# Weights loaded in 128-byte runs and turned by VectorE in a two-layer recurrent and attention kernel

## The reference

```python
xn = layernorm(x)
# layer 0: a recurrent mixer whose states start at zero
xi = xn @ W_in.T                                   # 512 x 256
y  = sum(C_real * B_real * xi - C_imag * B_imag * xi, axis=-1)
s  = xn + rmsnorm(y @ W_out.T) * norm_w
# layer 1: causal attention, qkv 256 x 768, o_proj 256 x 256
s  = softmax(mask(q @ k.T / 16)) @ v @ o_proj + xn # on layernorm(xn) * gamma + beta
# both layers: the gate, with H = 1024
g  = silu( fwht( silu(xn @ W1.T) * (xn @ W3.T) ) @ W2.T )
x  = x + s * g
```

## Time and profile before

| | |
|---|---|
| median of 3 runs | 363.39 us (362.97 to 363.65) |
| the profiled execution's own time | 363.3 us |
| its span | 361.5 us |
| what lies around the span | 1.8 us |
| TensorE busy | 355.8 us, 98% of the span |
| VectorE busy | 250.6 us, 69% |
| ScalarE busy | 169.2 us, 47% |
| GpSimd busy | 100.8 us, 28% |
| granted clock of TensorE | 0.999 of full speed |

### The profile page before, as it was taken

One profiled execution on the slowest core, in us unless ns is written; L12 is line 12 of the kernel. 1 busy time (PEld: TensorE's weight loads), 2 busy tenths in 40 slices (PEclk: granted clock), 3 DMA queues, 4 the chain that ended last, 5 costly groups with the idle time before them and its releaser, 6 DMA issues.

```text
span 361.5 us, 5052 instructions
## 1 busy us (share of the span) xinstructions
PE 355.8 (98%) x1821; PEld 301.5 (83%) x1821; DVE 250.6 (69%) x481; ACT 169.2 (47%) x335; POOL 100.8 (28%) x126
## 2 busy tenths in 40 slices
PE   7999999999999999999999999999999999999996
PEld 4878888888888888888988878888888888888896
DVE  5669965886489647868568894788646887356645
ACT  2865371355135623554275544644446354454510
POOL 2154410246014723467506030060300603004000
PEclk9999999999999999999999999999999999999999
DMA  7995110525145623440242401424204332054001
GB/s 239 287 320 198 60 59 0 176 58 170 35 133 159 190 74 117 120 145 0 72 134 67 141 0 60 151 54 126 81 30 160 74 117 88 0 190 111 20 3 58
DMA packets 42336, 38.63 MB, mean 107 GB/s; under 512 B 5700, under 2 KB 41800, under 8 KB 42312
## 3 DMA queue, kind: packets, MB, share of 16 engines
q1 hardware_dynamic: 42168, 38.25, 34.8%
q10 hardware_dynamic: 144, 0.07, 0.1%
HBM read 24.09 MB, written 14.22 MB: 106 GB/s over the span
## 4 chain that ended last, share of the span: by engine, by line
PE 94%; DMA 3%; DVE 1%; SPq 1%; issue 0%; ACT 0%
PE GU L362 19%; PE GU L363 19%; PE GU L364 19%; PE O L362 8%; PE O L363 8%; PE O L364 8%; DMA stage<-in_L_ffn_W 3%; PE O L369 1%; PE T L369 1%; PE O L433 1%; PE T L362 1%; PE T L364 1%; PE T L363 1%; PE O L519 1%; PE O L518 1%; PE O L517 1%
## 5 line engine op out<-in xcount | busy, mean ns | idle before, releaser
L730 ACT ACTIVATE hf<-GU 128x512 f32<-128x512 f32 x64 | 38.2, 599 | 80.3 <-DVE hid L854 55.8
L1001 DVE TENSOR_TENSOR hf<-hf,GU 128x512 f32<-128x512 f32 x64 | 43.6, 681 | 32.5 <-PE GU L364 27.1
L362 PE MATMUL GU<-XT,W1T 128*128 128x512 f32 x128 | 50.8, 397 | 0.0
L364 PE MATMUL GU<-XT,W1T 128*128 128x512 f32 x128 | 49.9, 390 | 0.0
L363 PE MATMUL GU<-XT,W1T 128*128 128x512 f32 x128 | 49.9, 390 | 0.0
L362 PE MATMUL GU<-XT,W3T 128*128 128x512 f32 x128 | 49.9, 390 | 0.0
L364 PE MATMUL GU<-XT,W3T 128*128 128x512 f32 x128 | 49.8, 389 | 0.0
L363 PE MATMUL GU<-XT,W3T 128*128 128x512 f32 x128 | 49.8, 389 | 0.0
L854 DVE TENSOR_TENSOR hid<-hf,hid 128x512 fp32r<-128x512 f32 x64 | 48.2, 754 | 1.2 <-ACT hid L661 0.8
L362 PE MATMUL O<-hid,W2hi 128*128 128x512 f32 x112 | 44.0, 393 | 0.0
L363 PE MATMUL O<-hid,W2hi 128*128 128x512 f32 x112 | 43.7, 390 | 0.0
(11 more groups left out here) (204 smaller groups left out, 741.2 us busy)
## 6 DMA issues: line engine op xcount, KB each, us to landing
stage<-in_L_ffn_W SPq DMA_DIRECT2D x24, 256.0 KB, 5.6
swap_rows<-GX SPq DMA_DIRECT2D x7, 512.0 KB, 3.6
sT<-swap_rows SPq DMA_DIRECT2D x28, 128.0 KB, 2.7
swap_gate<-GX SPq DMA_DIRECT2D x7, 512.0 KB, 2.9
sT<-swap_gate SPq DMA_DIRECT2D x28, 128.0 KB, 2.7
swap_p<-PX SPq DMA_DIRECT2D x4, 640.0 KB, 3.2
PL<-swap_p SPq DMA_DIRECT2D x16, 160.0 KB, 3.2
swap_w<-GX SPq DMA_DIRECT2D x4, 512.0 KB, 2.9
```

The lines of the kernel that those rows point to most:

```text
L362: pe.matmul(o, lhs(0), rhs(0), start=start, stop=False)
L364: return pe.matmul(o, lhs(1), rhs(0), start=False, stop=stop)
L730: act.activation(hf[:, c % 2, :], GU[:, c % 2, 0, :], ACT.Silu).then_inc(silu_done, 1)
L1001: dve.tensor_tensor(hf[:, c % 2, :], hf[:, c % 2, :], GU[:, c % 2, 1, :], ALU.mult).then_inc(mul_done, 1)
```

## The change

- W1 and W3 of pairs 1 to 7, W2 of layer 1, W_out and qkv are loaded by `load_blocks`: four DMAs for each, every one to 32 partitions, in runs of 32 numbers (128 bytes), so that the 32x32 blocks land where the transposed matrix has them. A W1 or W3 half of a pair is 4 DMAs of 512 runs, W_out 4 of 1024, qkv 4 of 1536 and W2 of layer 1 4 of 2048.
- VectorE then turns each block in place (`turn`, `turn_w2`, `turn_wout`, `turn_wqkv`; all of them instructions of L827). The transposes by TensorE of pairs 1 to 3 (W1, W3), of W_out and qkv and of layer 1's W2 are gone, and so are `w_turn`, `move_w` and `swap_w`. Pair 0 and the W2 of layer 0 stay as they were.
- GpSimd makes the lo parts of W1 and W3 from the stage (`pair_lo`, L1220) and those of layer 1's W2 (`nat_lo`, L1231); ScalarE makes the hi parts from SBUF.
- Nine small loads (five ssm arrays, W_in, norm_w, gamma, beta) are issued by ScalarE instead of SyncE. W_in is scaled by ScalarE.
- `small_m` comes after up chunk 7 in place of before it, `w2_hi` before the hi part of MR, layer 1's Hadamard matmuls stand after chunk 6 of groups 1 and 2 and after chunk 1 of groups 2 and 3, the butterflies of layer 1 in groups 2 and 3.
- SyncE loads the rest of X, pairs 4 and 5 and layer 1's W2 before the row exchange of group 1.

```diff
+            def load_blocks(to, src, done):
+                blocks = src.rearrange("(d b) (c q a) -> q b c d a", b=Q, q=QUADS, a=Q)
+                for q in range(QUADS):
+                    sp.dma_start(to[q * Q:(q + 1) * Q].rearrange("b (c d a) -> b c d a", d=D // Q, a=Q), blocks[q]).then_inc(done, 16)
...
+            def reload_w(i):
+                for w in (0, 1):
+                    sp.wait_ge(wx_lo, 2 * (i - 3) + w + 1)
+                    load_w(i, w)
...
+            reload_w(PAIRS)
+            reload_w(PAIRS + 1)
+            load_blocks(U2[1][:, :, :].rearrange("p c d -> p (c d)"), W2[1], w2_loaded)
             move_rows(1)
```

TensorE, the head and the groups of layer 0:

```diff
                 up_chunk(0, 0, 1, True)
-                head_hadamard(1)
-                head_pair(2)
-                head_pair_w2(2)
                 up_chunk(0, 0, 2, True)
+                hadamard(1)
+                pair_w2(2)
                 up_chunk(0, 0, 3, True)
-                head_hadamard(2)
-                head_pair(3)
-                head_pair_w2(3)
                 up_chunk(0, 0, 4, True)
+                hadamard(2)
+                pair_w2(3)
                 up_chunk(0, 0, 5, True)
-                head_hadamard(3)
-                small_natural()
+                hadamard(3)
+                small_gb()
                 up_chunk(0, 0, 6, True)
+                up_chunk(0, 0, 7, True)
                 small_m()
-                up_chunk(0, 0, 7, True)
                 small_av()
...
-                    if c == 2:
+                    if c == 1 and n > 1:
                         pe.wait_ge(gateT_ready, 2 * n)
-                        next_pair_w2(PAIRS + (0, 2, 3)[n - 1])
-                    if c == 4:
-                        next_hadamard(PAIRS + (0, 2, 3)[n - 1])
...
+                        hadamard(PAIRS + 2 * n - 3)
+                    if c == 6 and n < 3:
+                        pe.wait_ge(gateT_ready, 2 * n)
+                        hadamard(PAIRS + 2 * n - 2)
```

VectorE and ScalarE:

```diff
+            def in_place(part):
+                blocks = part.rearrange("p (f a) -> p f a", a=Q)
+                return dve.transpose(blocks, blocks)
+
+            def turn(i, w):
+                dve.wait_ge(stage_loaded[i % 2][w], landed(i))
+                in_place(stage[:, i % 2, w, :]).then_inc(w_turned, 1)
...
-                    last = dve.tensor_scalar(rows2[n % 2][:, t, :], X[:, bass.ds(x_at + t, 1), :].rearrange("p a d -> p (a d)"),
-                                             mv[:, t, 0:1], rstd[:, t:t + 1], ALU.subtract, ALU.mult)
+                    last = dve.scalar_tensor_tensor(rows2[n % 2][:, t, :], X[:, bass.ds(x_at + t, 1), :].rearrange("p a d -> p (a d)"),
+                                                    mv[:, t, 0:1], rstd[:, t:t + 1].broadcast_to([P, D]), ALU.subtract, ALU.mult)
...
+            def pair_hi(i):
...
+                    hi(WT[:, 0, :, cols], stage[:, i % 2, w, :].rearrange("p (k h) -> p k h", k=KC), w_turned, 2 * (i - 1) + w + 1, w_hi)
```

More of the change, by code:

```diff
@@ L164, in two_block_kernel, with landed @@
         xT = [[XT[:, a, k, :] for k in range(KC)] for a in (0, 1)]
[L165 to L177, removed]
+        def landed(i):
+            return 16 + 64 * (i // 2) if i % 2 == 0 else 64 * (i // 2 + 1)
         def blocks_of(a, c0, c1):
@@ L306, in _ @@
-            load_pair(0, 2, stage[:, 0, :, :], stage_loaded[0])
-            for i, m in enumerate((A_theta, B_real, B_imag, C_real, C_imag)):
-                sp.dma_start(ssm[:, i, :, :], m.rearrange("c (a p) s -> p (c a) s", p=P)).then_inc(small_loaded, 16)
-            sp.dma_start(win[:, :, :], W_in.rearrange("(a p) k -> p a k", p=P)).then_inc(small_loaded, 16)
-            sp.dma_start(wout[:, :, :], W_out.rearrange("(a p) n -> p a n", p=P)).then_inc(small_loaded, 16)
-            sp.wait_ge(w2_tr, 2)
@@ L397, in head_pair_w2, with pair_w2 @@
-            def head_pair_w2(i):
+                    pe.wait_ge(stage_loaded[0][w], 16)
+                    src = stage[:, 0, w, :].rearrange("p (a k) -> p a k", a=2)
+                    transposes(GU[:, 0, w, :], [src[:, a, k * P:(k + 1) * P] for k in range(KC) for a in (0, 1)]).then_inc(w_tr, 1)
+            def pair_w2(i):
                 if i:
                     pe.wait_ge(w2nat_ready, i)
-                pair_w2_transposes(i, stage[:, i % 2, :, :], stage_loaded[i % 2], 16 * (i // 2 + 1))
@@ L402, in next_pair_w2 @@
-            def next_pair_w2(i):
-                pe.wait_ge(w2nat_ready, i)
-                pair_w2_transposes(i, stage[:, i % 2, :, :], stage_loaded[i % 2], 16 * (i // 2 + 1))
-            def next_hadamard(i):
-                pe.wait_ge(u_ready, i)
-                pair_hadamard(i, w2nat)
-            def head_hadamard(i):
+                pe.wait_ge(stage_loaded[i % 2][2], 16 * (i // 2 + 1))
+                src = stage[:, i % 2, 2, :].rearrange("p (a h) -> p a h", a=2)
+                transposes(O[:, 0, :], [src[:, a, c * P:(c + 1) * P] for c in (0, 1) for a in range(KC)]).then_inc(w2_tr, 1)
@@ L420, in small_natural, with small_gb @@
+            def small_gb():
                 pe.wait_ge(small_loaded, 16 * N_SMALL)
[L421 to L423 removed]
                 pe.wait_ge(w2nat_ready, PAIRS)
@@ L679, in pair_u, with nat_hi @@
                 act.activation(U[l][:, 2 * j:2 * j + 2, :].rearrange("p a d -> p (a d)"), O[:, 1, :], ACT.Copy, scale=float(H) ** -0.5).then_inc(u_ready, 1)
-            def nat_hi(i, nat):
-                if not (isinstance(i, int) and i == 0):
+            def nat_hi(i):
+                if i:
                     act.wait_ge(h_done, i)
-                hi(nat[:, 0, :, :].rearrange("p a d -> p (a d)"), O[:, 0, :], w2_tr, i + 1, w2nat_hi)
-            def small_hi(first, n, wait, value, done):
-                for q in range(n):
-                    dst, src = first[q]
-                    hi(dst, src, wait, value + q, done)
+                hi(w2nat[:, 0, :, :].rearrange("p a d -> p (a d)"), O[:, 0, :], w2_tr, i + 1, w2nat_hi)
             def w2_hi(l):
```

328 lines of the change are left out of this document (156 added, 172 removed).

## The result

The changed kernel took 381.37 us (median of six runs, 380.0 to 384.65) against 363.33: 1.052 times as long (95% interval 1.046 to 1.057). Its profiled execution took 384.6 us by its own time, 21.3 more than that of before; it was one of the two longest of the six, so what is read from it lies some 3 us above the median.

A forecast was written before the change was run, and what follows sets the result against it. The prediction took TensorE, busy 98% of the span, as the bound. Waits of 9.6 us against a gain of 6.45 made +3.15, so 363.4 + 3.1 = 366.5 us, range 361.8 to 376.5.

The forecast's parts named there:

- lost in full: On TensorE: work removed from its program is won in full, each wait put into it lost in full.
- at about 52: SyncE's queue ahead of group 1's row exchange: through at about 52 us, at 0.84 ns a run, so in time.
- chain c: End of the head: small_av waits for VectorE's turns of qkv, 1.0 us (0 to 1.5).
- The gain, 6.45 us: TensorE: transposes removed and the wait for pair 3's late loads gone, 6.45 us saved; pair 1 counted as nothing.
- a: Head: up chunk 4 waits for chunk 2's mul, behind ScalarE's small loads, 2.6 us (0 to 6.5).
- D: Rival, chance 0.24: ScalarE's nine load issues in the head don't hold it, wait a is gone, 363.9 us.
- b: Head: pair 3's Hadamard matmuls wait for the lo part of W2, 1.7 us (1.0 to 2.3).
- if it took half the chains above would not change: VectorE's normalise beside up chunks 5 and 6: same time assumed; half that time would leave the waits unchanged.
- d: First mixer: waits 1.6 us for MR's lo part, then 0.5 for VR's; both together 1.0 to 3.0.
- e: Group 2: Hadamard matmuls after chunk 6 wait for GpSimd's lo part of W2, 2.2 us (1.2 to 3.5).
- rival B: Chance 0.15: short runs land late, group 1's up chunks wait for the row exchange; 372 us at 1.1 ns a run.
- A: The forecast itself, chance 0.54: short waits on TensorE outweigh the transposes saved, 365 to 368 us.

The follow-up runs named there:

- e7: e4 with ScalarE's nine small loads at the start of its program, right behind that of ident: 373.86 us (1.028).
- e5: e4 with GpSimd's butterflies of pair 3 in the head held until VectorE has normalised group 1's rows: 370.48 us (1.021).
- e4: Changed kernel with group 1's row exchange before layer 1's W2, layer 1's last butterflies back in group 4, GpSimd's lo parts first in group 2: 370.69 us (1.020).
- e9: Changed kernel with as many DMAs to the same tiles but in long contiguous runs, weights in the wrong places: 377.75 us (1.041).
- e13: Kernel before the change, with TensorE waiting in group 5 ahead of up chunk 5 for two small GpSimd instructions: 367.59 us (1.012).
- e14: Kernel before the change, with TensorE waiting in group 5 ahead of up chunk 5 for four small GpSimd instructions: 370.29 us (1.020).
- e8: e4 with the edits of e5 and e7, and TensorE's Hadamard matmuls of pair 3 and small_gb behind up chunk 6: 372.12 us (1.025).
- e10: e4 with VectorE's five turns of W_out and qkv cut to 32 columns each, those weights staying unturned: 370.71 us (1.021).
- e16: e15 with the lo parts of pairs 1 to 3 made by VectorE instead of GpSimd: 376.12 us (1.033).
- e1: Changed kernel with SyncE moving group 1's rows before it loads layer 1's W2, not after: 378.83 us (1.043).
- e3: Changed kernel with GpSimd making pair 6's lo parts and those of its W2 before the butterflies in group 2: 379.23 us (1.044).
- e15: e4 with MR's hi part ahead of W2hi on ScalarE and its lo part ahead of U's sums on VectorE: 370.26 us (1.020).

## Why the prediction was wrong

The sign and the main mechanism (waits that outweigh the transposes) were right: all five waits that it named are in the profile. The size was not, 18.0 us in place of 3.1, and 381.4 lies outside the range. Of the steps that failed these are the largest: each wait was "lost in full" at its length and no more, with no term for TensorE's clock (up to 6.5 us); the queue was to be through "at about 52", so that the row exchange cost nothing (3.6); no step priced the butterflies beside group 3's normalise (3.1); and chain c took VectorE as free at the end of up chunk 7 (2.4). The sizes are those of the profiled execution, which lies 3.3 us above the median. By the prediction's steps:

- **The gain, 6.45 us**: mis-sized by 1.5 or more, as far as the profiles show. The account leaves 5.3 us or less for what TensorE no longer does. Without pair 1's 0.8, which this gain didn't count, and with the 0.4 of listed waits for pair 3's loads, that is 4.9 or less.
- **a** (2.6): 1.0 in the profile. ScalarE's ssm loads took 0.39 to 0.65 each, and began while it still worked on w2nat. They did hold the silu of chunk 1, so D was wrong too, and e7, without them there, lost this wait.
- **b** (1.7): 2.6. Not priced were VectorE's lo part beside GpSimd (1.62 in place of 0.6) and a load of x that came 0.36 late.
- **c** (1.0): 2.0, and small_m 1.4 more, which I had at nothing. The step that failed is "if it took half the chains above would not change", said of the normalise. The earlier trace rows had no row for it. That it takes the same time was not the error: it had 5.90 us in the head before and has 4.71 now. But in the new order the turns of W_out and qkv stand behind it, so VectorE comes late to chain c. In e5 it took 1.67, and the chain did change: the turns of W_out ended at 38.5 in place of e4's 41.3, and small_av waited 1.4 in place of 2.0.
- **d** (1.6 + 0.5): 1.2 + 0.4.
- **e** (2.2): 3.7. The 512-wide instructions of GpSimd took 1.44 to 1.63 beside VectorE; my upper bound of 3.5 had named that.
- **Group 3's normalise**, a wait of 3.1: no step of mine spoke of it. I had told that the butterflies move to group 3 and priced them only in group 2. It took 1.34 us there before and 5.70 now.
- **The exchange (rival B, 0.15)**: happened, a wait of 3.6. My 0.84 ns a run was the DMA engines' time in a quiet stretch. In the queue it took 14.40 us for 8192 runs, 1.76 ns each, some 3 us of which (an estimate, at 365 GB/s) are 1 MB of x ahead of them, and 7.10 us for the next 8192, 0.87 ns each; the queue was through at 59.8, not at 52. e9 shows that the runs made it so.
- **The clock**, up to 6.5 us: the missing term. e13 and e14 show 1.9 and 2.6 us beside waits of 2.7 and 4.7. In the changed kernel's profile it stands behind the waits of groups 1 to 3, not in the head.

Without the clock, the exchange and group 3 the sum would be 381.4 - 6.5 - 3.6 - 3.1 = 368.2, near A's own range. What stays open is how the rest of the head's loss divides: e4's seven microseconds sit in waits whose relief, one at a time, moved them on (e5, e8, e10, e16), and no run relieved all at once.

## What to carry to other kernels

On an engine that is busy 98% of the time a wait costs its length and then, in most of these profiles, a stretch at half clock; price both. Another wait close behind can take the stretch up, as in the head of e4. When work moves to an engine that was idle, look at what its neighbour does at that time, and at which of the neighbour's instructions have both inputs in SBUF: VectorE's normalise grew from 1.6 to 5.7 us with GpSimd beside it, while turns and muls kept their time. And follow a queue in program order to the first transfer that the bound engine needs: 8192 short runs ahead of it were all that it took.

## What the runs showed of the hardware

- VectorE's four normalise instructions of 128x256 took 1.62 to 1.67 us alone, and 4.69 to 5.75 beside GpSimd's butterflies; as tensor_scalar 1.34 to 1.38 alone and 4.22 to 5.90 beside them. Turns and the mul, with an operand in PSUM, kept their time beside them (1.29 for two, 0.65). The lo part, both inputs in SBUF, ended 0.54 to 0.55 us after GpSimd's instruction in three profiles.
- Idle time of 2.7 and 4.7 us on TensorE was followed by stretches at granted clock 0.50, which cost another 1.9 and 2.6 us. Behind pair 3's wait (2.5 to 2.9 us) the clock fell in the profiles of e1, e4, e5 and e10 and not in that of the changed kernel; behind group 3's wait of 3.1 it fell in those of the changed kernel and of e1, and not in e3's.
- Half clock costs little where another wait takes it up: e4's executions took 370.2 to 370.9 us at a mean granted clock of 1.000, and 370.8 at 0.991; e15's 369.7 and 369.9 at 0.999, and 370.6 and 371.1 at 0.989 to 0.991.
- A DMA of 2048 runs of 128 bytes took 1.78 us of SyncE's queue, one with the same bytes in long runs 0.45.
